# Scores three quads in advance and 32 row buffers in a graph kernel on one core

## What is computed

```python
h = maximum(layernorm(x), 0)
fwd = segment_sum(w * h[col, :128], row) / clip(deg_row, 1)      # layer 0, phase S
bwd = segment_sum(w * h[row, 128:], col) / clip(deg_col, 1)      # layer 0, phase D
x = x + concat(fwd, bwd)
def gat(x, W, b, a, g, beta):                                    # one attention layer
    h = x @ W.T + b
    score = (h @ a[:d])[src] + (h @ a[d:])[dst]
    e = exp(-leaky_relu(score, 0.2))
    y = segment_sum(e[:, None] * h[dst], src)
    return layernorm(y) * g + beta
h = maximum(layernorm(x), 0)
z = concat([elu(gat(h, head i)) for 8 heads of 64])              # attention 1
x = x + elu(gat(z, W_out, ...))                                  # attention 2, output
```

## Time and profile before

| | us |
|---|---|
| median of 3 runs | 3398.36 (3397.92 to 3401.51) |
| the profiled execution | 3428.28 |
| its span | 3426.5 |
| granted TensorE clock, mean | 0.816 of full |
| POOL busy in the span | 1937.1 (57%) |
| TensorE / VectorE / ScalarE busy | 2456.6 / 2052.3 / 1769.0 |

### The profile page before, as it was taken

One profiled execution on the slowest core, in us unless ns is written; L12 is line 12 of the kernel. 1 busy time (PEld: TensorE's weight loads), 2 busy tenths in 40 slices (PEclk: granted clock), 3 DMA queues, 4 the chain that ended last, 5 costly groups with the idle time before them and its releaser, 6 DMA issues. The chain is left out here.

```text
span 3426.5 us, 49940 instructions
## 1 busy us (share of the span) xinstructions
PE 2456.6 (72%) x16596; PEld 1844.4 (54%) x16596; DVE 2052.3 (60%) x4366; ACT 1769.0 (52%) x5198; POOL 1937.1 (57%) x2009
## 2 busy tenths in 40 slices
PE   7898889789886898434477777777766565656652
PEld 3787778778876787333343333333335444444441
DVE  7997778678766787222365666665677233333337
ACT  2786677667765777222233343433438344444445
POOL 1002666666666666666645656555546566666663
PEclk7998899889887999555588988888887777777776
DMA  1010111111132111211445556555540333333343
GB/s 58 1 40 16 41 44 43 45 42 44 44 43 46 44 44 44 53 46 47 47 124 160 163 161 167 163 165 162 162 103 26 87 89 90 90 89 89 89 87 60
DMA packets 114898, 270.71 MB, mean 79 GB/s; under 512 B 34543, under 2 KB 51670, under 8 KB 114646
## 3 DMA queue, kind: packets, MB, share of 16 engines
q0 software_dynamic: 89088, 245.53, 29.3%
q1 hardware_dynamic: 25558, 21.98, 2.0%
HBM read 250.96 MB, written 16.42 MB: 78 GB/s over the span
## 5 line engine op out<-in xcount | busy, mean ns | idle before, releaser
L401 POOL DMA_INDIRECT rows_near<-table_a,s_idx_S x464 | 470.6, 1014 | 309.2 <-issue 112.5
L401 POOL DMA_INDIRECT given<-table,s_idx_S x464 | 446.0, 961 | 298.8 <-issue 124.6
L401 POOL DMA_INDIRECT rows_near<-table,s_idx_S x464 | 446.9, 963 | 280.8 <-issue 128.9
L1101 DVE TENSOR_TENSOR work<-work,bank 128x129 f32 (+2 forms) x928 | 390.0, 420 | 343.2 <-remote 168.3
L401 POOL DMA_INDIRECT rows_near<-table_b,s_idx_D x464 | 453.7, 978 | 237.5 <-issue 113.5
L768 PE MATMUL bank<-rows_near,oh 128*128 128x129 f32 x1856 | 348.8, 331 | 236.0 <-issue 130.0
L893 PE MATMUL bank<-scratch,oh 128*128 128x512 f32 x928 | 491.4, 679 | 5.1 <-issue 3.5
L754 PE MATMUL bank<-scratch 128*128 128x224 bf16 (+1 forms) x2520 | 423.4, 277 | 61.8 <-issue 40.7
L768 PEld LDWEIGHTS bank<-rows_near,oh 128*128 128x128 f32 x1856 | 288.7, 230 | 278.2 <-issue 218.3
L600 ACT ACTIVATE e_att<-lrelu 128x32 f32<-128x32 f32 (+1 forms) x232 | 49.9, 215 | 737.4 <-DVE lrelu L1258 488.9
L754 PE MATMUL bank<-rows_near,sort_ring 128*128 128x224 bf16 (+1 forms) x2520 | 408.2, 271 | 27.2 <-issue 18.8
(11 more groups left out here) (216 smaller groups left out, 4636.0 us busy)
## 6 DMA issues: line engine op xcount, KB each, us to landing
rows_near<-table_a,s_idx_S POOLq DMA_INDIRECT x464
rows_near<-table_b,s_idx_D POOLq DMA_INDIRECT x464
rows_near<-table,s_idx_S POOLq DMA_INDIRECT x464
given<-table,s_idx_S POOLq DMA_INDIRECT x464
table<-scratch SPq DMA_DIRECT2D x25, 260.0 KB
table<-scratch SPq DMA_DIRECT2D x25, 128.5 KB, 2.8
xs<-in_x SPq DMA_DIRECT2D x1, 3072.0 KB
out_x<-scratch SPq DMA_DIRECT2D x24, 128.0 KB, 1.7
```

What stands on the lines that cost most here:

```text
L401: nc.gpsimd.indirect_dma_start(out=to, out_offset=None, in_=table[:, :], in_offset=bass.IndirectOffsetOnAxis(ap=s_idx[order][:, c:c + 1], ...
L1101: v.tensor_add(a, a, psum).then_inc(sum_free[o], 1)
```

## The change

**Rows.** Layer 0 has 32 row buffers (16 more, `more_rows0`, in `scratch2`), with a semaphore for each; POOL waits for the chunk 32 before instead of 16. It has eight half-bank sums instead of six, and adds three quads later (two from `FIRST` + 2 on). One-hots stay at 16 chunks. Attention 2 has 32 row buffers too, attention 1 keeps 16.

**Attention.** The order becomes `messages(q)`, `scores(q + 1)`, `add_groups(q - 2)` on VectorE; transposes of quad q + 5 and source scores of q + 3 before `sums(q)` on TensorE; `weights(q + 1)`, the eviction of transposes q + 4 and of scores q + 2, and one-hots q + 6 on ScalarE. Scores share the two banks of the transposes and are copied to SBUF (`s_edge`) by ScalarE, so VectorE reads them from there. Sum banks are 2 to 7. One-hots have eight quads of buffers, transposes four, messages three.

**Output.** Statistics and (x - mean) x gain are done beside the sums of attention 2 (`beside_sums`), the square root in two parts. After them, per tile: x 1/std plus offset (held in PSUM) in one VectorE operation, elu through PSUM (ScalarE, VectorE), the residual on POOL.

**Smaller.** Four staging buffers and four landing semaphores for each table instead of two; the transposes and features of the blocks of phase D alternate between banks 0 and 1; the means of a block in one operation per tile instead of two for the block.

The core of the diff:

```diff
@@ -56,7 +56,14 @@
 
 FIRST = next(q for q in range(QUADS) if tiles_done(2 * q + 2))
 BLOCKS = [range(tiles_done(2 * q), tiles_done(2 * q + 2)) for q in range(FIRST, QUADS)]
-SUMS0 = 6
+SUMS0 = 8
+ROWS0 = 2 * SLOTS
+ROWS2 = 2 * SLOTS
+OH_QUADS = 8
+OHT_QUADS = 4
+SUMS = 6
+AHEAD = {"oh": 6, "turn": 5, "evict": 4, "score": 3}
+EARLY = BLOCKS[-3].stop
 assert tiles_done(GROUPS) == T and all(1 <= len(b) <= 2 for b in BLOCKS) and len(BLOCKS) < 16
...
+            return bank[n % 2][:, (t - BLOCKS[n].start) * 2 * HEADS:(t - BLOCKS[n].start + 1) * 2 * HEADS]
+
+        def row0(n):
+
+            return (rows0 if n % ROWS0 < SLOTS else more_rows0)[:, n % SLOTS, :]
...
+                        pool.wait_ge(rows_made, 1)
+                    if n >= ROWS0:
+                        pool.wait_ge(chunks_summed, n + 1 - ROWS0)
+                    gather(table, row0(n)[:, 0:HALF], order, c, gathered[n % ROWS0])
 
             def gather_layer1(o, table, width):
                 for c in range(CHUNKS):
                     if c >= SLOTS and o == "1":
                         pool.wait_ge(msg_ready[o], c + 1 - SLOTS)
-                    elif c >= SLOTS:
-                        pool.wait_ge(sum_ready[o], (c - SLOTS) // GP + 1)
-                    gather(table, row_slots(c % SLOTS, 1)[:, 0, 0:width], "S", c)
+                    elif c >= ROWS2 and o == "2":
+                        pool.wait_ge(sum_ready[o], (c - ROWS2) // GP + 1)
+                    gather(table, row_slots(o, c, 1)[:, 0, 0:width], "S", c, landing(o, c)[0])
 
...
             for t in range(T):
-                pool.wait_ge(scaled, t + 1)
-                nc.gpsimd.tensor_tensor(work[:, t, 0:C], work[:, t, 0:C], betao[:, :], ALU.add).then_inc(offset_added, 1)
+                pool.wait_ge(z_done, t + 1)
+                if t >= 4:
+                    pool.wait_ge(q_out[t % 4], 16 * (t // 4))
+                nc.gpsimd.tensor_tensor(final[:, t % 4, :], work[:, t, 0:C], xs[:, t, :], ALU.add).then_inc(final_ready, 1)
...
+                    if q >= OH_QUADS:
+                        act.wait_ge(sum_ready[o], 2 * (q - OH_QUADS) + 2)
...
+                def evict(turn, score):
+
+                    act.wait_ge(turn_psum[o], turn + 1)
+                    if turn < QUADS:
+                        nc.scalar.activation(ohT[:, turn % OHT_QUADS, :], turned[turn % 2], ACT.Copy).then_inc(ohT_ready[o], 1)
+                    if 0 <= score < QUADS:
+                        if score >= 4:
+                            act.wait_ge(z_ready[o], score - 3)
+                        n = QUAD * heads
+                        nc.scalar.activation(s_edge[:, score % 4, 0:n], selected[score % 2][:, 0:n], ACT.Copy).then_inc(ssrc_ready[o], 1)
...
+                for q in range(-AHEAD["oh"], QUADS):
+                    if 0 <= q + 1 < QUADS:
+                        weights(q + 1)
+                    turn = q + AHEAD["evict"]
+                    if 0 <= turn < QUADS + AHEAD["turn"] - AHEAD["score"]:
+                        evict(turn, turn + AHEAD["score"] - AHEAD["turn"])
+                    if q + AHEAD["oh"] < QUADS:
+                        one_hots(q + AHEAD["oh"])
...
+            nc.scalar.copy(offset_row, betao[:, :]).then_inc(offset_in_psum, 1)
+            for a, b in ((0, EARLY), (EARLY, T)):
+                act.wait_ge(moments_ready, 2 * T + b)
+                nc.scalar.activation(rstd[:, a:b], mv[:, a:b, 1], ACT.Sqrt, bias=eps[:, :]).then_inc(std_ready, 1)
+            for t in range(T):
+                elu_exponential(t)
...
+                for q in range(-AHEAD["turn"], QUADS):
+                    turn, score = q + AHEAD["turn"], q + AHEAD["score"]
+                    if score >= 0 and score % 4 == 0 and score < QUADS:
+                        tiles = tile_numbers(mybir.EngineType.PE, "S", TILE_AT + 2 * score, min(8, GROUPS - 2 * score))
+                    if score < QUADS:
+                        if turn >= 2 and turn < QUADS + 2:
+                            pe.wait_ge(ohT_ready[o], turn - 1)
+                        if score >= 2:
+                            pe.wait_ge(ssrc_ready[o], score - 1)
+                        if turn < QUADS:
+                            last = transposed(turn)
+                        if score >= 0:
+                            last = source_scores(score, tiles[score % 4 * 2:score % 4 * 2 + 2])
+                        last.then_inc(turn_psum[o], 1)
+                    if q >= 0:
+                        sums(q)
...
@@ -1089,7 +1137,9 @@
 
             def one_hots(o, phase, q):
 
-                dve.wait_ge(chunks_summed, phase * CHUNKS + q * QUAD + QUAD)
+                n = phase * CHUNKS + (q + 1) * QUAD
...
             def add_sums(o, phase, q, tiles):
 
-                dve.wait_ge(chunks_summed, SLOTS + phase * CHUNKS + QUAD * (q + 1))
+                dve.wait_ge(chunks_summed, phase * CHUNKS + QUAD * (q + 1))
...
             def layer0(o, phase, between):
 
...
+                    lag = 3 if q < FIRST + 2 else 2
+                    while added <= q - lag:
+                        if added % 4 == 0:
+                            tiles = tile_numbers(mybir.EngineType.DVE, o, TILE_AT + 2 * added, min(8, GROUPS - 2 * added))
+                        add_sums(o, phase, added, tiles[added % 4 * 2:added % 4 * 2 + 2])
+                        added += 1
...
+            def beside_sums(q):
+
+                n = q - FIRST - 2
+                if 0 <= n - 1 < len(BLOCKS):
+                    for t in BLOCKS[n - 1]:
+                        dve.wait_ge(moments_ready, 2 * T + t + 1)
+                        v.scalar_tensor_tensor(out=work[:, t, 0:C], in0=work[:, t, 0:C], scalar=mv[:, t, 0:1], in1=go[:, :],
+                                               op0=ALU.subtract, op1=ALU.mult).then_inc(gained, 1)
+                if 0 <= n < len(BLOCKS):
+                    dve.wait_ge(sum_free["2"], SUMS + 2 * (FIRST + n + 1))
+                    for t in BLOCKS[n]:
+                        v.bn_stats(stats[:, t, :], work[:, t, 0:C]).then_inc(stats_ready, 1)
+                    for t in BLOCKS[n]:
+                        tile_moments(t, 2 * T)
...
-                dve.sem_inc(sum_free[o], 4)
+                dve.sem_inc(sum_free[o], SUMS)
...
+                def scores(q):
 
...
                     n = QUAD * heads
                     dve.wait_ge(ssrc_ready[o], q + 1)
                     for k in range(QUAD):
-                        b = u % UNROLL * QUAD + k
-                        dve.wait_ge(gathered[b], i * 16 + 16 * ((1 + int(o)) * ROUNDS + 1 + u // UNROLL))
-                    v.tensor_tensor(score[:, u % 2, 0:n].rearrange("p (k h) -> p k h", h=heads),
-                                    bank[2 + u % 2][:, 0:n].rearrange("p (k h) -> p k h", h=heads),
-                                    row_slots(u % UNROLL * QUAD, QUAD)[:, :, width:width + heads], ALU.add).then_inc(z_ready[o], 1)
+                        dve.wait_ge(*landing(o, q * QUAD + k))
+                    v.tensor_tensor(score[:, q % 2, 0:n].rearrange("p (k h) -> p k h", h=heads),
+                                    s_edge[:, q % 4, 0:n].rearrange("p (k h) -> p k h", h=heads),
+                                    row_slots(o, q * QUAD, QUAD)[:, :, width:width + heads], ALU.add).then_inc(z_ready[o], 1)
...
+                for q in range(QUADS + 2):
+                    if q % 4 == 0:
+                        tiles = tile_numbers(mybir.EngineType.DVE, "S", TILE_AT + 2 * q - 4, min(8, GROUPS + 4 - 2 * q))
+                    if q < QUADS:
+                        messages(q)
+                    if q + 1 < QUADS:
+                        scores(q + 1)
+                    if q >= 2:
+                        add_groups(q - 2, tiles[q % 4 * 2:q % 4 * 2 + 2])
+                    if o == "2":
+                        beside_sums(q - 1)
...
             def finish(t):
+                dve.wait_ge(exp_ready, t + 1)
                 y = work[:, t, 0:C]
-                elu(t, t % 2, y).then_inc(z_done, 1)
-                dve.wait_ge(z_done, t + 1)
-                if t >= 4:
-                    dve.wait_ge(q_out[t % 4], 16 * (t // 4))
-                v.tensor_tensor(final[:, t % 4, :], y, xs[:, t, :], ALU.add).then_inc(final_ready, 1)
-
...
+                v.scalar_tensor_tensor(out=y, in0=neg_exp[t % 4], scalar=-1.0, in1=y, op0=ALU.add, op1=ALU.max).then_inc(z_done, 1)
+
+            for q in range(QUADS + 1, QUADS + 3):
+                beside_sums(q)
+            dve.wait_ge(offset_in_psum, 1)
+            for n, a, b in ((0, 0, EARLY), (1, EARLY, T)):
+                dve.wait_ge(std_ready, 2 + len(BLOCKS) + n)
+                link(v.reciprocal(rstd[:, a:b], rstd[:, a:b]))
+                for t in range(a, b):
+                    dve.wait_ge(gained, t + 1)
+                    y = work[:, t, 0:C]
+                    v.scalar_tensor_tensor(out=y, in0=y, scalar=rstd[:, t:t + 1], in1=offset_row, op0=ALU.mult, op1=ALU.add).then_inc(offset_added, 1)
```

(3 more changed lines are left out.)

282 lines of the change are left out of this document (119 added, 163 removed).

## The result

The changed kernel took 3452.2 us (3441.1 to 3461.7, four runs) beside 3399.7 for the kernel before (3397.9 to 3401.5): a ratio of 1.0167 with a 95% interval of 1.0142 to 1.0192. It is 1.7% slower; forecast were 3260 us, range 3110 to 3370.

What follows compares the result with a forecast made beforehand. Attention was taken as bound by POOL stopping because TensorE's results come late while it streams gathers. Gains 50 + 40 + 15 + 10 + 3 + 19 = 137 us off 3398.4 gave 3261, rounded to 3260; range 3110 to 3370.

Steps and rivals of the forecast that it cites:

- The cycle: Attention: POOL streams, VectorE runs out of TensorE's results, POOL stops, results arrive; a lead of about one quad counts.
- the failed step: Layer 0 while sorting: TensorE, VectorE and the ring of two sorted batches set the pace; 32 buffers cost nothing.
- 15 + 10 + 3: Layer 0 gains in us: 15 after the first direction's last merge, 10 without sorting, 3 for blocks of tiles and tables.
- The third rival: Sorting stretches: ring stalls more often, 58 more stops of 5.0 us, adding 290 us, giving 3550; chance 0.06.
- the second term that failed: Attention 1: one quad more of lead, 3.4 quads per stop instead of 2.4, gains 50 us; bounds 0 and 155.
- Attention 2: 32 row slots and more lead: a stop every 2.15 quads instead of 1.15; 50 us less 10, gain 40.
- the second rival: Lead is used up: POOL's stops get rarer but proportionally longer; only output, merge and tables gain, 3361 us; chance 0.15.
- its own sign: Sign of the second rival: POOL's wait per quad stays above 0.9 us in both attentions.
- Output: Output stage: 55.9 us becomes 37, with POOL as the pace at 1.05 us per tile; gain 19 us.
- The longer end of attention 2: With up to 32 rows waiting, more is left after the last gather of attention 2; 10 us taken back.

Runs made afterwards that it cites:

- the pauses in the slow session: Changed kernel with POOL waiting before each eighth gather of layer 0 until the previous one landed; slow session: 3510.1 us, 1.0226 of the kernel before.
- run 7: Changed kernel with 16 row buffers in layer 0 instead of 32, slow session: 3387.9 us, 0.9984 of the kernel before.
- run 11: Changed kernel with 16 row buffers in layer 0 and one quad less of lead in attention, slow session: 3456.1 us, 1.0073 of the kernel before.

## Why the prediction was wrong, point by point

**What bounds the kernel.** The cycle (POOL streams, TensorE's results come late, POOL stops, the results come) was right for the trace that was read, and the pauses in the slow session bear part of it out: the 43 us hold became 11.6. "All at once" is not what the trace of TensorE shows: it starts its instructions late itself, every 0.70 us or a multiple, so the results are late and not only late to be seen. And the cycle was taken for a property of the kernel. It is one of the session: in free sessions it doesn't exist, and POOL's issue is the bound in layer 0 and both attentions, where it never pauses.

**Layer 0, the failed step.** "While sorting ... I cost the 32 buffers at nothing there" and a gain of 15 + 10 + 3 behind it. Measured: +71.5 us in the two traces; 71 us between 32 and 16 buffers in two slow sessions (1534.9 and 1463.9), 59 us within one (1529.6 and 1470.9). I asked only whether POOL is a bound. The question to ask was what POOL's extra lead displaces. In the slow session TensorE hardly moved late in a long stream of gathers (busy 4.1 of the 24 us from 347 to 371); 16 more gathers ahead are 16 x 1.25 = 20 us of issuing before the same sums, and the sort's wait at the start of phase S grew by 23.5 us (19.87 to 43.41). That would be repaid later, if POOL could use its lead. It can't: the lead ends at a barrier, the merge. There POOL waits 28.0 us instead of 3.3 [the two gathers after merges above], for a sort that has come later by the holds.

POOL's gathers are a blurred measure of where the 71 us went, since POOL is now further ahead. The last operation of each merge (L1087, now L1135) stands at 315, 664, 1013 and 1378 us before and at 320, 684, 1065 and 1443 after: the three sorting stretches lost 15, 33 and 13 us and the rest of layer 0 11. VectorE's waits for the ring in these stretches went from 69, 54 and 46 us to 90, 103 and 64. In the first two it is the one long wait (19.87 us became 43.41, and 39.31 is new); in the third no wait is over 6 us, and it is the short ones that grew. That the buffers are the cause, and no other edit in layer 0, is shown (run 7 keeps the others and is as long as before); that the exchange works in this way is argued from the traces. At the end of layer 0 the same shows as the tail, 75.3 instead of 56.8: POOL is done, and the blocks of tiles, 5.7 us each, are still to come.

**The third rival** had the right place, the right sign and the wrong mechanism. It priced short holds of 5.0 us at every second batch. The waits put down to "remote" in the earlier trace rows are 28 before and 28 after; with those put down to TensorE the ring's waits are 55, 170 us, before (of which the earlier trace rows shows 135) and 53, 257 us, after. The number stayed; two long holds came. Only in the third sorting stretch do short waits make the loss, as this rival had it. Its 172 batches should be 168, of which 126 are sorted beside gathers. 0.06 was a small chance for an edit costed at "nothing" in the stretch where TensorE is at 87%.

**Attention 1, the second term that failed**, -50 forecast, -22 measured. The lead did lengthen the cycle, to 2.9 quads (3.4 assumed), but the stop grew from 3.5 to 3.9 us, where I had kept its length: (3.94 - 0.30)/2.9 = 1.25 us per quad instead of 0.94. The count of 45 stops left out 13 short ones that the profile puts down to "issue". With them POOL stopped 60 times in the 464 gathers, once in 1.9 quads and for 3.0 us, and after the change 39 times, once in 3.0 quads and for 4.0 us: one quad more, as forecast, and one microsecond longer, as not. The lead itself works (32 us, run 11).

**Attention 2**, -40 forecast, -7 measured. One stop per 2.06 quads, almost exactly the 2.15 assumed; but 2.06 us each instead of 1.36. (2.06 - 0.30)/2.06 = 0.85 us per quad against 0.92, times 116 is 8. A little over half as many stops, each half as long again: so "stops are rarer but proportionally longer", the second rival, was nearly right here. By its own sign (above 0.9 us of waiting per quad in both attentions) it lies between: 1.25 and 0.85. What goes with the longer stops can be seen in TensorE's waits from 1500 to 3400 us, first before, then after (total, times, longest):

```profile
PE bank L878 <- ACT scratch L596: 322.2, 83, 9.8
PE bank L878 <- issue: 26.9, 22, 3.8
```

```profile
PE bank L928 <- issue: 266.3, 283, 2.0
```

Before, TensorE stood at its score products because ScalarE had no transposes. Now it has them, and stands there all the same, 283 times, with nothing to wait for: it works off its lead at the slow pace. The kernel after in a free session has no such wait at all. A lead lets work start sooner, but here it didn't make it faster, since it was the issue that was slow.

**Output**, -19 forecast, -25.5 measured (55.9 to 30.4). The pace is 13.01/18 = 0.72 us per tile, not 1.05: POOL's additions run back to back without the 0.30 of gathers. The Trainium skill ("SBUF — State Buffer", section "SBUF: two separate sides") has VectorE and GpSimd exclude each other where VectorE reads two SBUF inputs and GpSimd reads SBUF. The traces agree: 0.83 us beside POOL with two SBUF inputs before, 0.42 and 0.47 with one of them in PSUM after. The longer end of attention 2 took back 15 us (last gather to last sum 30.1 instead of 14.8), not 10. Together -10.2.

**Numbers.** Forecast 137 us of gain; the two traces show a loss of 30. Of the 167 us between, layer 0 with its tail is 99 (+71.5 instead of -28) and attention with its longer end 76 (-14 instead of -90); the start adds 5, and the output stage and the dense part come out 13 better than forecast. By medians the loss is 53 us, so another 23 us are in no stretch of the table. Nor would the forecast have held without the 32 buffers: run 7, whose layer 0 is as long as before, is level with the kernel before by medians (5 us, within the measurement).

## What to carry to other kernels

More buffers are not free by rule: here a producer that ran further ahead took time from the others first, and since its lead ended at a barrier it could not be used. Look for the barrier, and ask what is idle while the producer waits at it. And before a wait that the profile can't name is made the ground of a forecast, take a second trace of the same kernel in another session: here one from a free session would have shown that the same program has two bounds. And when an edit makes a stream longer, look for the longest wait in the trace beside today's stream: the 19.87 us were there to be read.

## What the runs showed of the hardware

- One program, unchanged, took 2976 to 2985 us in four sessions and 3393 to 3432 in three others, one chip in both kinds. In free sessions POOL issued indirect gathers without a pause, one per 1.25 to 1.32 us.
- In slow sessions TensorE has stretches beside POOL's gathers in which it starts an instruction every 0.70 us (or two to four times that), though it waits for nothing. In the stream from 320.8 to 371.6 such a stretch began 24 us in and ended some 5 us after POOL had stopped (371.6 and 377); in the kernel before it was 24 us and 4 us (316.2, 340, 346.7 and 350.5). VectorE waits for the result all that time. In the two traces of free sessions it was so 2 times and never, with the same gathers.
- What makes a session slow was not found. The transfers are not longer: a packet of the gathers' queue takes 0.161 us at the median in slow and free traces of the kernel before alike, and one of the 16 KiB packets of a queue of kind "instruction" 1.03 us in the slow and 1.07 us in the free one. It was not tried either whether the DMA traffic or POOL's own work is what TensorE suffers from: the run with memsets fell into free sessions both times.
